# Attention with heads of 16: the turned scores issued one piece at a time between the plain pairs

## The reference

```python
q = _ln((x @ Wq + bq).reshape(b, s1, H, HD), qn_w, qn_b)       # b=2, s1=128, H=16, HD=16
k = _ln((y_main @ Wk + bk).reshape(b, s2, H, HD), kn_w, kn_b)  # s2=2032
v = (y_main @ Wv + bv).reshape(b, s2, H, HD)
s = jnp.einsum('bhqd,bhkd->bhqk', q, k) * SCALE
p = jax.nn.softmax(s, axis=-1)
ctx = jnp.einsum('bhqk,bhkd->bhqd', p, v)
ctx = ctx + attention of the last 16 rows, with weights of their own
out = ctx @ Wo + bo
```

## Time and profile before

| | |
|---|---|
| median of 3 runs | 1298.5 us |
| lowest and highest | 1297.9 and 1305.51 us |
| the profiled execution | 1297.31 us |
| its span, first to last instruction | 1295.6 us |
| mean granted TensorE clock | 0.959 of 2.4 GHz |
| first and last plain or turned matmul of the 32 steps | 410.5 and 512.2 us into the span |

### The profile page before, as it was taken

How to read it: one execution, slowest core, us unless ns; L and a number is a source line. 1 busy time by engine, 2 the same in 40 slices (tenths; PEclk the granted TensorE clock), 3 DMA queues, 4 the chain that set the end, 5 groups by cost and what they waited for, 6 DMA issues and landing times. The chain is left out here.

```text
span 1295.6 us, 23108 instructions
## 1 busy us (share of the span) xinstructions
PE 1146.9 (89%) x8738; PEld 761.3 (59%) x8742; DVE 992.0 (77%) x1858; ACT 860.9 (66%) x1303; POOL 317.5 (25%) x353
## 2 busy tenths in 40 slices
PE   7999999848776887899899999887998999999987
PEld 3677676635322444486566666645874666666644
DVE  6788878297768883493899989776987998998654
ACT  5777778484454887422877777565976777777563
POOL 3000000100362000000172654502650456275200
PEclk8899999959986999899899999999998999999999
DMA  7999999201374000901899999514745999999600
GB/s 280 172 186 189 188 171 187 84 1 74 82 146 82 2 3 2 245 25 59 162 200 182 206 182 169 130 43 160 205 115 129 180 181 183 178 163 169 123 1 9
DMA packets 450833, 170.00 MB, mean 131 GB/s; under 512 B 437160, under 2 KB 437544, under 8 KB 449064
## 3 DMA queue, kind: packets, MB, share of 16 engines
q1 hardware_dynamic: 450736, 168.72, 62.3%
HBM read 58.84 MB, written 0.26 MB: 46 GB/s over the span
## 5 line engine op out<-in xcount | busy, mean ns | idle before, releaser
L462 PE MATMUL ps<-ctxT,L_xattn_qk 128*128 128x512 f16 x1152 | 270.3, 385 | 0.8 <-DVE L_xattn_mx L742 0.5
L766 DVE SCALAR_TENSOR_TENSOR arena<-L_xattn_sm,L_xattn_rr,arena 128x1024 f16<-128x1024 f32 x192 | 260.9, 1399 | 9.4 <-ACT arena L612 9.4
L597 ACT ACTIVATE L_xattn_sm<-L_xattn_sm,L_xattn_mx 128x2048 f32<-128x2048 f32 x96 | 192.3, 2003 | 75.6 <-DVE L_xattn_mx L742 73.9
L612 ACT ACTIVATE arena<-L_xattn_sm,L_xattn_rr 128x1024 f16<-128x1024 f32 x192 | 210.0, 1140 | 5.2
L462 PEld LDWEIGHTS ps<-ctxT,L_xattn_qk 128*128 128x128 f16 x1152 | 112.5, 99 | 130.1 <-issue 9.9
L484 PE MATMUL ps<-arena,ctx 128*128 128x256 f16 x1488 | 177.7, 273 | 0.0
L484 PEld LDWEIGHTS ps<-arena,ctx 128*128 128x128 f16 x1488 | 145.4, 98 | 31.9
L742 DVE CUSTOM_DVE_ANT_0 L_xattn_sm<-ps,L_xattn_bias 128x1024 f32<-128x1024 f32 x96 | 117.0, 1219 | 55.7 <-issue 55.5
L742 DVE CUSTOM_DVE_ANT_0 L_xattn_sm<-ps,L_xattn_bias,L_xattn_mx 128x1024 f32<-128x1024 f32 x96 | 123.2, 1284 | 2.4 <-DVE L_xattn_mx L742 2.1
L475 PE MATMUL ps<-arena,ctx 128*128 128x128 f16 x1488 | 100.8, 222 | 9.6 <-DMA arena<-arena 9.5
L475 PEld LDWEIGHTS ps<-arena,ctx 128*128 128x128 f16 x1488 | 92.3, 99 | 25.1 <-DMA arena<-arena 13.4
(11 more groups left out here) (585 smaller groups left out, 2082.7 us busy)
## 6 DMA issues: line engine op xcount, KB each, us to landing
L_ffn_ring<-in_L_ffn_experts SPq DMA_DIRECT2D x34, 384.0 KB, 3.6
arena<-in_L_xattn_w SPq DMA_DIRECT2D x36, 320.0 KB, 3.7
arena<-in_L_ffn_experts SPq DMA_DIRECT2D x8, 768.0 KB, 7.7
arena<-in_L_xattn_w SPq DMA_DIRECT2D x6, 640.0 KB, 6.5
arena<-arena SPq DMA_TRANSPOSE x193, 4.5
arena<-in_L_ffn_codes SPq DMA_DIRECT2D x1, 3072.0 KB, 11.2
arena<-in_L_attn_w SPq DMA_DIRECT2D x1, 2163.0 KB, 19.3
arena<-in_L_attn_w SPq DMA_DIRECT2D x2, 1026.0 KB, 5.1
```

What stands on the lines that cost most here:

```text
L462: last = nc.tensor.matmul(ps[:, at, :], qk[:, h // 2, qp, h % 2, b * P:(b + 1) * P], k.ctxT[:, cp, b, at * 512:(at + 1) * 512], start=(a = ...
L597: nc.scalar.activation(sm[:, u % 2, :], sm[:, u % 2, :], ACT.Exp, bias=mx[:, u % 2, 1:2], scale=-1.0, accum_out=rs[:, u % 2:u % 2 + 1]).th ...
L612: nc.scalar.mul(pp[:, u % 2, 0, at], sm[:, u % 2, at], rr[:, u % 2:u % 2 + 1]).then_inc(s.p_high, 1)
L766: nc.vector.scalar_tensor_tensor(pp[:, u % 2, 1, at], sm[:, u % 2, at], rr[:, u % 2:u % 2 + 1], pp[:, u % 2, 0, at], ALU.mult, ALU.subtrac ...
```

## The change

`scores_turned` takes one piece `j` in place of a pair. It waits for its own bank alone (the exponential of piece-3), issues the four matmuls of one head, all on the same half of the rows, and signals. The pair's eight matmuls had alternated between the two halves. In the loop the order becomes: extras, piece 0, plain pair 0, piece 1, plain pair 1, piece 2, `mix` 0, piece 3, `mix` 1. So the extras and one piece now stand ahead of plain pair 0, and one piece stands between plain pair 1 and `mix` 0. The number of matmuls, their sizes, the banks and all work of ScalarE and VectorE stay.

```diff
-                def scores_turned(step, pair):
+                def scores_turned(step, j):
 
                     G, at = step // 4, step % 4
-                    b, a = G // 4, 2 * (G % 4) + pair
-                    if at == 0 and pair == 0:
+                    b, a, which = G // 4, 2 * (G % 4) + j // 2, j % 2
+                    if at == 0 and j == 0:
                         pe.wait_ge(s.m_set, 2 * G + 2)
-                    first = 4 * step + 2 * pair
-                    for piece in (first, first + 1):
-                        if piece >= 3:
-                            pe.wait_ge(s.p_ready, piece - 2)
+                    piece = 4 * step + j
+                    if piece >= 3:
+                        pe.wait_ge(s.p_ready, piece - 2)
                     for i in range(4):
-                        for which in range(2):
-                            last = nc.tensor.matmul(ps[:, ST_BANK[(first + which) % 3], i * P:(i + 1) * P],
-                                                    ks[b][half(which), 4 * at + i, a, :], qs[half(which), b, a, :],
-                                                    start=True, stop=True)
-                            if i == 3:
-                                last.then_inc(s.st_ready, 1)
+                        last = nc.tensor.matmul(ps[:, ST_BANK[piece % 3], i * P:(i + 1) * P],
+                                                ks[b][half(which), 4 * at + i, a, :], qs[half(which), b, a, :],
+                                                start=True, stop=True)
+                    last.then_inc(s.st_ready, 1)
+
+                def scores_ahead(step, first, end):
+
+                    if step + AHEAD < STEPS:
+                        scores(4 * (step + AHEAD) + first, 4 * (step + AHEAD) + end)
@@ the loop @@
                     G, at = step // 4, step % 4
-                    if step + AHEAD < STEPS:
-                        scores(4 * (step + AHEAD), 4 * (step + AHEAD) + 2)
                     if step == 1:
                         turn_last()
@@
                     scores_turned(step, 0)
-                    if step + AHEAD < STEPS:
-                        scores(4 * (step + AHEAD) + 2, 4 * (step + AHEAD) + 4)
+                    scores_ahead(step, 0, 2)
+                    scores_turned(step, 1)
+                    scores_ahead(step, 2, 4)
+                    scores_turned(step, 2)
                     if step:
                         mix(step - 1, 0)
-                    scores_turned(step, 1)
+                    scores_turned(step, 3)
                     if step:
                         mix(step - 1, 1)
```

## The result

The changed kernel took 1318.9 us (median of 6 runs, 1312.6 to 1322.0) against 1299.6 us for the kernel before (1297.9 to 1305.5): a ratio of 1.0136, 95% interval 1.0111 to 1.0161. That is 19 us slower between the medians and 17.7 us by the ratio. A second set of runs of the same kernel gave 1.0142 (1.0102 to 1.0181). The forecast was 1313.0 us (+14.5), the range 1299 to 1321, and slower by over 1% the likeliest outcome (0.49).

A forecast was written before the change was run, and what follows sets the result against it. The loop was taken as bound by hand-offs among TensorE, VectorE and ScalarE, the first reduction tying each step. Terms +2.9 (steps 0 to 3), +10.7 (five sets), +0.3, +1.2 and -0.6 gave +14.5, 1313.0 us; range 1299 to 1321.

The forecast's parts named there:

- The chain: Loop step from plain pair 0 through its first reduction, plain pair 1, pieces and `mix`: 3.42 us, 0.44 above 2.98.
- The price of a piece: Four turned matmuls on one half of the rows cost 0.22 us, the same as the alternating pair.
- rival 4: Much slower: weight loads of the loop's single pieces not hidden, 30 us more, 1343; chance 0.05.
- The extras: Turning of maxima and mixed output, now ahead of plain pair 0, joins the chain: steps of 3.95 and 4.15 us.
- ScalarE's slack: Exponentials gain a bank of slack, but ScalarE did not bound the step; only the last five steps gain, -0.6 us.
- The sum: Whole kernel: start, sets, `turn_out`, late steps and last five steps add to +14.5 us, giving 1313.0.
- Six sets: Loop sets of four steps grow from 12.81 to 14.94 us, +2.13 each.
- Start: Loop steps 0 to 3, partly at the lower clock, with pieces and extras in the chain: together +2.9 us.
- Tail: Last five steps, without plain scores and bound by ScalarE, gain from the slack: -0.6 us.
- The faster one: Plain pair 1 need not stand for the reduction, so TensorE's own order sets the step: 1288 us; chance 0.12.
- The third: About the same: pieces 0 and 2 hide in the change of shapes around `mix`, +2.6, 1301; chance 0.18.

The follow-up runs named there:

- e2: Changed kernel with single pieces in the order of before: plain pair 0 ahead of extras and piece 0, piece 2 behind `mix` 0; ratio 0.9998.
- e1: Changed kernel with only the extras moved back behind plain pair 0; ratio 1.0030.
- e3: Like e2 against the changed kernel, but piece 2 stays ahead of `mix` 0; ratio 1.0019.
- e5: e2 with the extras moved behind piece 1; ratio 0.9957.
- e6: Kernel before, pairs and their waits kept, with the extras moved behind turned pair 0; ratio 0.9959.
- e7: Changed kernel with seven unused 512-column matmuls in TensorE's wait ahead of the loop; median 1312.0 us, ratio 1.0109.
- e0: Changed kernel run again unedited for a second profile; median 1318.3 us, ratio 1.0142.
- e8: e5 with plain pairs parted into single tasks, each behind its own bank's wait, task 2 ahead of the extras, task 3 behind `mix` 0; 1286.8 us, ratio 0.9915.
- e4: e2 with both plain pairs parted into single tasks, each behind its own bank's wait, task 3 behind `mix` 0; ratio 1.0006.
- e9: e8 with seven unused 512-column matmuls in TensorE's wait ahead of the loop; ratio 0.9908.

## Why the prediction was right, and where it was short

**The chain.** Right, and to a hundredth: S01, reduction, S23, T2, `mix` 0, T3, `mix` 1, T0. The step was priced at 3.42 and measures 3.41 to 3.42 (its terms as printed add to 3.43). The four steps of a set, from the first plain matmul of each, are 3.41 (`at` 3 to 0, 457.02 to 460.44), 4.13, 3.41 and 3.95, against 3.42, 4.15, 3.42 and 3.95. The set is 14.90 against 14.94.

**The price of a piece.** Right: four matmuls on one half take 0.38 to 0.40 from first start to last end, which is three slots (128 columns each) of 0.056 and a last matmul of 0.216, with a load into the same rows for each. The rule of the Trainium skill, page "TensorE: Matmul & The Clock Gate", section "Part 3: Packing small matmuls — row/col tiling", that a load overlaps a matmul in flight only if their row groups differ, would by itself have given 0.60 and rival 4, and here the trace disagrees with it; the same section also has a load into a background weight buffer pulled ahead of matmuls in flight, and that the trace agrees with. What the forecast left out is that pieces of both halves run side by side even when one is issued behind the other. That made e2 free, and it changes nothing in the changed kernel, where T0 and T2 have no free neighbour of the other half in front of what the chain waits for.

**The extras.** Right in kind and size: 1.25 of the 2.09 a set is their move ahead of S01 (e1), 0.90 is T0 (e1 against e3), and the remaining 0.27 for T2 (e3 against e2) less 0.33 that single pieces in the old order gain (e2 against before) is -0.06; 1.25 + 0.90 - 0.06 = 2.09. The saving at `at` 3 to 0 that was forecast (the 6.1 us of the earlier trace rows) is in there.

**ScalarE's slack.** Right that it doesn't bound the step. The finer waits are worth 0.33 a set in the old order and nothing once the extras are out of the way (e5 against e6).

**Where it was short.** The sum was +14.5, the layer grew by 19.0 in the trace (191.6 to 210.6) and the kernel by 17.7 (ratio) to 19 (medians). Held against the sum's terms, all measured between the turnings of the maxima:
- Six sets: 90.1 against 77.0, +13.2; forecast 6 x 2.13 and 0.3 for `turn_out`, +13.1. `turn_out` cost 0.75 and not 0.3 (the set with it is 15.65), made up by a first set that was 12.95 before.
- Start, up to the second turning: 15.4 against 10.9, +4.6; forecast +2.1 at this point (the +2.9 were for S01 of step 3, which stood 0.4 ahead of the turning before and was to stand 0.4 behind it). This term was mis-sized. It priced only steps 0 and 1 at the lower clock, as if the clock rose where it had before, at 416 us; it rose at 424.
- Tail: 22.3 against 21.0, +1.3; forecast -0.6. The steps there ran at 0.50 for 7 us, from 523 to 530. With the full clock (e7) the tail is 20.6, -0.4.

So 4.4 of the 4.5 us of shortfall in the layer lie in the two stretches where the clock was at the lower level, the same in both profiles of the changed kernel, and the trace of e7 shows both gone from the layer when TensorE is kept at work before the loop (its next such stretch begins at 532.3 us, behind the layer).

For the kernel as a whole the second stretch counts less. The kernel before has one too, from 518.2 to 525.0 us, and it falls on the head of the next layer. The thirteen matmuls there, before and changed:

```profile
519.45 5.71 PE L180 MATMUL ps<-ctxT,identh 128*128 128x512 f16 x13 [1.27 <-PEq L2232]
...
539.57 4.65 PE L180 MATMUL ps<-ctxT,identh 128*128 128x512 f16 x13 [1.27 <-PEq L2232]
```

1.1 us of the 19.0 are given back there, which leaves 18.0, with 3.5 of shortfall: 2.5 in the start, and under 1 in the tail. In e7 it is 11.7; the difference, 6.3, is near the 6.2 between the medians of e0 and e7. (The two profiled executions, 1297.3 and 1321.2 us, differ by 23.9. Of that 1.1 lies ahead of the layer and 4.8 behind it, in layers that no edit touches; behind it the profiles of the experiments differ from that of the kernel before by -0.4 to +5.8.)

What holds the clock down at the start is shown in part. The kernel before and e1 wait as long ahead of the loop as the changed kernel (3.2 us), so that wait alone isn't it; e1 differs from the changed kernel only in the place of the extras, and its clock is up 7 us sooner. That the idle time and the thinner steps 0 and 1 do it together is what the rows suggest; why the fall at 523 comes was not tried apart.

**The rivals.** The faster one hung on S23 not having to stand for the reduction; it stood 24 times of 24. With that wait removed, in another order, e8 has sets of 11.08, near the 11.2 that the rival had said; the orders differ, so this doesn't confirm the rival's sum. The third (pieces hidden in the change of shapes) fell with the 0.22 and 0.31 of the timeline.

## What to carry to other kernels

Before an order is refined, find the one wait in the loop that has no slack, and write down what stands in TensorE's stream between its release and the next time it is armed. Here what was put there was paid nearly in full: 0.90 a set for one piece (0.88 by its streams) and 1.25 for the extras, against the 0.33 at most that the finer waits of the turned scores brought. And the wait itself, which asks for a pair where a single would do (S23), was worth 0.95 a set once nothing else held the step. An edit that removes the wrong wait can cost (e4) and pay later (e8), so try it again once the bound has moved.

## What the runs showed of the hardware that was not expected

- Matmuls of different halves of the rows don't start strictly in the order of issue. In the changed kernel T0 (four matmuls, lower half), task 0 (lower), task 1 (upper) are issued in this order, and one plain matmul starts at 457.02, between the second and the third of T0, the other at 457.18. Two pieces issued one behind the other took 0.41 together (e2), and in the last steps three pieces in a row, T0, T1 and T2, took 0.62, eight slots and the run-out:

```profile
517.29 0.62 PE L2377 MATMUL ps<-arena,L_xattn_ks 64*128 64x128 f16 x12
```

- Work in a wait of 3.3 us ahead of a loop changed the clock far behind it. In the changed kernel the lower level held for 24 us, 12 of them in the loop; with seven matmuls in that wait for 10 us, and it was over before the loop began. But a stretch at the lower level came again at the layer's end or behind it in every kernel, at 518 us in the kernel before, at 508 in e9 and at 536 in e8. Where it fell on the thirteen matmuls at the head of the next layer they took up to 5.7 us (the kernel before), where it did not, 3.0 (e8).
